# A fused attention and FFN layer: a second ALiBi buffer in place of a third score buffer, and all weight loads on one queue

## What is computed

```python
xn = _layernorm(x)
x = x + attn(xn) + ffn(xn)
# attn, H=16 heads of D=64, T=2048
q, k, v = split(xn @ W_attn + b_attn)
att = (q @ k.T) / sqrt(D) / temperature
att = att + where(causal, slopes[h] * (pos_k - pos_q), -inf)
y = softmax(att) @ v
attn = y @ W_proj + b_proj
# ffn, HIDDEN=3072, int32 weights scaled by 1/127
ffn = (silu(xn @ wg.T) * (xn @ wu.T)) @ wd.T
```

## Time and profile before

| | us |
|---|---|
| time, median of 3 runs | 2096.98 (2095.66 to 2149.68) |
| time of the profiled execution | 2096.67 |
| its span on the slowest core, core 7 | 2095.1 |
| spans of the eight cores | 2070.9 to 2095.1 |
| stage 4 on core 7, from the first score matmul | 1077.9 to 2095.1 |
| TensorE busy on core 7 | 1344.0 |
| VectorE busy | 947.5 |
| ScalarE busy | 923.0 |

### The profile page before, as it was taken

One profiled execution on the slowest core, in us unless ns is written; L12 is line 12 of the kernel. 1 busy time (PEld: TensorE's weight loads), 2 busy tenths in 40 slices (PEclk: granted clock), 3 DMA queues, 4 the chain that ended last, 5 costly groups with the idle time before them and its releaser, 6 DMA issues.

```text
span 2095.1 us, 26200 instructions; the slowest of 8 cores (2070.9 to 2095.1 us)
## 1 busy us (share of the span) xinstructions
PE 1344.0 (64%) x8642; PEld 700.7 (33%) x8642; DVE 947.5 (45%) x1601; ACT 923.0 (44%) x1745; POOL 78.8 (4%) x148
## 2 busy tenths in 40 slices
PE   0000059899898998089976566656656565666666
PEld 0000024344343443034334334334334343432333
DVE  2335321010110110244138686868768686855663
ACT  2335333022031230000248786877777676853442
POOL 0000000000000000023000000000000000000000
PEclk9955579999999999589985555555555555557877
DMA  8878544244243431722210101010100101012212
GB/s 241 269 259 266 169 151 141 81 147 135 77 165 101 133 128 41 257 74 77 85 41 1 61 1 61 1 61 1 51 11 1 61 1 61 1 71 81 81 61 91
DMA packets 46188, 198.87 MB, mean 95 GB/s; under 512 B 6119, under 2 KB 6120, under 8 KB 38378
## 3 DMA queue, kind: packets, MB, share of 16 engines
q1 hardware_dynamic: 31402, 142.67, 21.3%
q0 software_dynamic: 14080, 48.24, 6.3%
q10 hardware_dynamic: 576, 6.29, 0.8%
HBM read 157.34 MB, written 39.85 MB: 94 GB/s over the span
## 4 chain that ended last, share of the span: by engine, by line
PE 50%; DMA 16%; DVE 12%; issue 12%; ACT 9%; DVEq 0%; SPq 0%; ACTq 0%; POOL 0%; POOLq 0%
PE ps_dn L405 8%; PE ps_g L361 8%; PE ps_u L369 8%; PE ps_tr L775 7%; DVE snegp L663 6%; PE ps_qk L492 5%; ACT ptb L739 4%; ACT pbuf L699 4%; PE ps_y L800 4%; PE ps_tr L876 3%; PE ps_v L528 3%; DMA abcp<-alibi_bc 3%; PE ps_s L644 3%; DMA wistage<-wd_r 2%; DVE ncmx L625 2%
## 5 line engine op out<-in xcount | busy, mean ns | idle before, releaser
L663 DVE SCALAR_TENSOR_TENSOR snegp<-ps_s,abcp 128x1024 f32<-128x1024 f32 (+2 forms) x320 | 330.6, 1058 | 246.6 <-PE ps_s L650 246.6
L739 ACT ACTIVATE ptb<-ps_tr 128x512 bf16<-128x512 f32 (+3 forms) x640 | 313.4, 531 | 265.9 <-PE ps_tr L775 261.2
L775 PE MATMUL ps_tr<-ident_s,pbuf 128*128 128x128 bf16 x2176 | 290.1, 296 | 186.8 <-ACT ptb L739 90.1
L625 DVE TENSOR_REDUCE ncmx<-snegp 128x2 f32<-128x1024 f32 (+2 forms) x320 | 328.4, 1052 | 3.5
L699 ACT ACTIVATE pbuf<-snegp,negmax 128x128 bf16<-128x128 f32 (+15 forms) x256 | 305.2, 1195 | 41.1 <-DVE negmax L680 38.9
L775 PEld LDWEIGHTS ps_tr<-ident_s,pbuf 128*128 128x128 bf16 x2176 | 191.4, 128 | 303.3 <-issue 292.3
L644 PE MATMUL ps_s<-k_hp,q_hp 64*128 64x512 bf16 (+2 forms) x320 | 142.8, 506 | 162.1 <-DVE snegp L663 94.4
L405 PE MATMUL ps_dn<-wdres,hbuf 128*128 128x512 bf16 x768 | 177.0, 391 | 38.4 <-DVE xfout L426 32.9
L361 PE MATMUL ps_g<-xnT,wgbuf 128*128 128x512 bf16 x768 | 182.8, 381 | 8.7 <-DMA wubuf<-wu_sc 7.8
L295 PE MATMUL ps<-ident_s,xn_st 128*128 128x128 bf16 x128 | 16.2, 305 | 263.7 <-DVE xn_st L278 263.7
L369 PE MATMUL ps_u<-xnT,wubuf 128*128 128x512 bf16 x768 | 181.4, 379 | 0.0
(11 more groups left out here) (65 smaller groups left out, 1030.0 us busy)
## 6 DMA issues: line engine op xcount, KB each, us to landing
wgbuf<-wg_sc SPq DMA_DIRECT2D x48, 512.0 KB
wubuf<-wu_sc SPq DMA_DIRECT2D x48, 512.0 KB
abcp<-alibi_bc SPq DMA_DIRECT2D x16, 1024.0 KB
wistage<-wg_r SPq DMA_DIRECT2D x12, 1024.0 KB
wistage<-wu_r SPq DMA_DIRECT2D x12, 1024.0 KB
wistage<-wd_r SPq DMA_DIRECT2D x12, 1024.0 KB
xstage<-xin SPq DMA_DIRECT2D x16, 512.0 KB
x2st<-xin POOLq DMA_DIRECT2D x16, 512.0 KB, 5.4
```

The source lines that it names most:

```text
L625: cd = S.op("vector", lambda e, par=par, c0=c0, w=w, ci=ci: e.tensor_reduce(ncmx[:, par * 8:par * 8 + 8].rearrange("p (j c) -> p j c", j=2 ...
L663: stt = S.op("vector", lambda e, par=par, hb=hp % 2, aoff=aoff, c0=c0, w=w, rA=rA: e.scalar_tensor_tensor(snegp[par].rearrange("p (j t) -> ...
L739: return e.activation(dst, src, AF.Copy)
L775: lasttr = S.op("tensor", lambda e, par=par, j=j, kc=kc, slot=slot, idx=idx, n=len(kcs): e.matmul(ps_tr[:, slot * 512 + (kc % 4) * 128: sl ...
```

## The change

Four edits.

- All eight wattn loads are issued on SP; the ScalarE queue and its two semaphores go.
- `snegp` has two buffers instead of three, by s % 2. The addition of step s waits for the exp of s-2 instead of s-3. The small tiles (ncmx, negmax, sumr, rsum) stay with three.
- `abcp` has two buffers, by hp % 2. The load of pair hp waits for the last addition recorded for the buffer's former pair, hp-2.
- The early load of q and k of the first pair waits for all stores of q and k and for `p3_pe`, the last V matmul. The tensors have moved by 16 KB in SBUF.

```diff
-                    ld = S.dma("sync" if wb == 0 else "scalar",
-                        lambda e, dc=dc, wb=wb: e.dma_start(
+                    ld = S.dma("sync", lambda e, dc=dc, wb=wb: e.dma_start(
                         out=wst3[wb][:, :], in_=wattn[dc * 128:(dc + 1) * 128, :]),
...
-            snegp = [E4b(nc.sbuf_tensor(f"snegp{p}", [128, 2 * T], F32, side="right")) for p in range(3)]
+            snegp = [E4b(nc.sbuf_tensor(f"snegp{p}", [128, 2 * T], F32, side="right")) for p in range(2)]
...
-            sneg_rel = [0, 0, 0]
+            sneg_rel = [0, 0]
...
                 if early:
                     wts = [wat_fin, qk_st_war[2], qk_st_war[3]]
-                    wq = [wat_fin] + store_of_fc[0] + store_of_fc[8]
+                    wq = qk_st_fin + [("pe", p3_pe)]
                 else:
-                    wts = [("v", abc_war[0])]
+                    wts = [("v", abc_war[hb])]
...
-                l1 = S.dma("sync", lambda e, hp=hp: e.dma_start(
-                    out=abcp0[:, 0:T], in_=alibi_bc[2 * hp, :, :]), waits=wts)
+                l1 = S.dma("sync", lambda e, hp=hp, hb=hb: e.dma_start(
+                    out=abcp[hb][:, 0:T], in_=alibi_bc[2 * hp, :, :]), waits=wts)
...
-                    if sneg_rel[par]:
-                        wts2.append(("a", sneg_rel[par]))
+                    if sneg_rel[sp]:
+                        wts2.append(("a", sneg_rel[sp]))
...
-                    abc_war[0] = S.c("v")
+                    abc_war[hp % 2] = S.c("v")
...
-                sneg_rel[par] = ed
+                sneg_rel[pb] = ed
...
-            abcp0 = E4b(nc.sbuf_tensor("abcp0", [128, 2 * T], F32, side="right"))
-            abcp = [abcp0, abcp0]
+            abcp = [E4b(nc.sbuf_tensor(f"abcp{i}", [128, 2 * T], F32, side="right")) for i in range(2)]
```

More of the change, by code:

```diff
@@ L29 @@
 class KB:
-    QSEMS = {"sync": ("dl0", "dl1"), "gpsimd": ("dg0", "dg1"),
-             "scalar": ("ds0", "ds1")}
+    QSEMS = {"sync": ("dl0", "dl1"), "gpsimd": ("dg0", "dg1")}
     def __init__(self, nc, block, sem):
@@ L40, in __init__ @@
         self.waited = {e: {} for e in ENGS}
-        self.qidx = {"sync": 0, "gpsimd": 0, "scalar": 0}
+        self.qidx = {"sync": 0, "gpsimd": 0}
     def dma(self, queue, fn, waits=()):
@@ L120, in build_program @@
         sem = {s: E(nc.semaphore("sem_" + s)) for s in
-               ("dl0", "dl1", "dg0", "dg1", "ds0", "ds1", "pe", "v", "a")}
+               ("dl0", "dl1", "dg0", "dg1", "pe", "v", "a")}
         block = E(nc.Block())
@@ L551, in build_program @@
             E4b = s4b.enter_context
-            snegp = [E4b(nc.sbuf_tensor(f"snegp{p}", [128, 2 * T], F32, side="right")) for p in range(3)]
-            sneg = [[snegp[p][:, j * T:(j + 1) * T] for j in range(2)] for p in range(3)]
+            snegp = [E4b(nc.sbuf_tensor(f"snegp{p}", [128, 2 * T], F32, side="right")) for p in range(2)]
+            sneg = [[snegp[p][:, j * T:(j + 1) * T] for j in range(2)] for p in range(2)]
             pbuf = [[E4b(nc.sbuf_tensor(f"pbuf{p}_{j}", [128, T], BF16, side="right")) for j in range(2)] for p in range(2)]
@@ L600, in emit_group_load @@
                     wq = [("pe", qk_war[hb])] if qk_war[hb] else []
-                l1 = S.dma("sync", lambda e, hp=hp: e.dma_start(
-                    out=abcp0[:, 0:T], in_=alibi_bc[2 * hp, :, :]), waits=wts)
-                l2 = S.dma("sync", lambda e, hp=hp: e.dma_start(
-                    out=abcp0[:, T:2 * T], in_=alibi_bc[2 * hp + 1, :, :]))
+                l1 = S.dma("sync", lambda e, hp=hp, hb=hb: e.dma_start(
+                    out=abcp[hb][:, 0:T], in_=alibi_bc[2 * hp, :, :]), waits=wts)
+                l2 = S.dma("sync", lambda e, hp=hp, hb=hb: e.dma_start(
+                    out=abcp[hb][:, T:2 * T], in_=alibi_bc[2 * hp + 1, :, :]))
                 l3 = S.dma("sync", lambda e, hp=hp, hb=hb: e.dma_start(
@@ L614, in emit_scores_softmax @@
                 par = it % 3
+                sp = it % 2
                 ch = chunks_of(L)
@@ L624, in emit_red @@
                     ci, c0, w, dep = pend_red.pop(0)
-                    cd = S.op("vector", lambda e, par=par, c0=c0, w=w, ci=ci: e.tensor_reduce(
+                    cd = S.op("vector", lambda e, par=par, sp=sp, c0=c0, w=w, ci=ci: e.tensor_reduce(
                         ncmx[:, par * 8:par * 8 + 8].rearrange("p (j c) -> p j c", j=2)[:, :, ci:ci + 1],
-                        snegp[par].rearrange("p (j t) -> p j t", j=2)[:, :, c0:c0 + w],
+                        snegp[sp].rearrange("p (j t) -> p j t", j=2)[:, :, c0:c0 + w],
                         AX.X, AluOpType.max),
@@ L659, in emit_scores_softmax @@
                         wts2 += group_ld[hp % 2][0:2]
-                    if sneg_rel[par]:
-                        wts2.append(("a", sneg_rel[par]))
+                    if sneg_rel[sp]:
+                        wts2.append(("a", sneg_rel[sp]))
                     aoff = T - 128 + c0 - qt * 128
-                    stt = S.op("vector", lambda e, par=par, hb=hp % 2, aoff=aoff, c0=c0, w=w, rA=rA: e.scalar_tensor_tensor(
-                        snegp[par].rearrange("p (j t) -> p j t", j=2)[:, :, c0:c0 + w],
+                    stt = S.op("vector", lambda e, sp=sp, hb=hp % 2, aoff=aoff, c0=c0, w=w, rA=rA: e.scalar_tensor_tensor(
+                        snegp[sp].rearrange("p (j t) -> p j t", j=2)[:, :, c0:c0 + w],
                         ps_s[:, rA:rA + 1024].rearrange("p (j t) -> p j t", j=2)[:, :, 0:w],
@@ L699, in emit_exp @@
                     ed = S.op("scalar", lambda e, par=par, pb=pb, j=j, L=L: e.activation(
-                        pbuf[pb][j][:, 0:L], sneg[par][j][:, 0:L], AF.Exp,
+                        pbuf[pb][j][:, 0:L], sneg[pb][j][:, 0:L], AF.Exp,
                         bias=negmax[:, par * 2 + j: par * 2 + j + 1],
```

## The result

The changed kernel takes 2056.31 us as the median of ten executions, the kernel before 2097.69 (ten, taken beside them). The ratio is 0.9795, 95% interval 0.9781 to 0.9809: 2.05% faster. The forecast was 2059 us. On either side some executions are several per cent longer whatever the kernel does; all ratios leave these out, a median over all executions does not. The two medians alone stand at 0.9803, so which side of 2% the gain falls on is not settled.

A forecast was written before the change was run, and what follows sets the result against it. The prediction took ScalarE's idle at seven pair changes, with scores waiting for k, as the loss to remove: 2096.67 - 40.9 + 5.0 - 2.0 = 2058.8, so 2059 us, range about 2050 to 2070.

The forecast's parts named there:

- The stall at the change of pair: Seven pair changes in attention: second abcp buffer removes the k_hp waits and most of ScalarE's idle, gaining 40.9 us.
- snegp: Bias additions in attention: with two buffers the wait for exp(s-2) is already covered by VectorE's earlier reciprocals, cost 0.
- The price without cover: Rival in attention: additions wait for the previous step's exp, exposing up to 305.2 us, up to 2364 us; chance 3%.
- The start: Start of attention: q and k of pair 0 wait for the last V matmul, delaying the first score, cost 5.0 us.
- wattn: W_attn loads all on SP: second load follows sooner (-1.4 us), loads then 4.9 us apart; -2 us in all.
- The 2% mark: Whole run: faster by over 2% begins below 2055 us, given 27%; within 2% given 70%.
- The differences between cores gone: Sign expected in the profile: first to last score about 925 to 928 us on every core, without differences between cores.
- The clock rival: TensorE in attention: without the 9.3 us holes its clock rises to 2.4 GHz, at most 115 us, 1944 us; chance 3%.

The follow-up runs named there:

- e3: The changed kernel with a single abcp buffer again, addresses kept by an unused tile: 2097.75 us, ratio 1.0004 to the kernel before.
- e4: The kernel before, with q and k issued on SP ahead of the two ALiBi loads in each pair's load: 2055.95 us, ratio 0.9804.
- e9: e4, with q and k of the next pair also waiting for the last addition: ratio 0.986 to the kernel before (0.982 to 0.990).
- e10: The changed kernel run once more, unaltered, beside e11 and e12: ratio 0.9831 to the kernel before.
- e5: The changed kernel with tiles reordered so q and k of pair 0 load during V: 2054.87 us, ratio 0.981 to the kernel before.
- e11: e5 run again, unaltered, beside e10: ratio 0.9842 to the kernel before.
- e12: e4 with all wattn loads on SP: ratio 0.9812 to the kernel before.
- e1: The kernel before with two snegp buffers instead of three, addresses kept by an unused tile: ratio 1.0005 to the kernel before.
- e6: The changed kernel with a single snegp buffer: 2240.13 us in a single execution.

## Why the prediction was right, by its steps

- *The stall at the change of pair.* Its mechanism held at each point: seven waits for k gone, ScalarE idle 0.53 us instead of 6.1 to 7.2, TensorE still idle before the transposes (3.29 us). e3 brings the stall back, e4 and e9 show that the path ran through exp, transposes and copies and that TensorE's idle as such was free. The size was 40.9 forecast from core 7. ScalarE's idle at the seven changes fell by 40.9 as a mean over cores, and the attention stretch by 42.6. The six kernels with the short attention and an unchanged body (changed, e10, e4, e5, e11, e12) lie at 927.8 to 930.7, so the 1.7 us are within what the column scatters, and whether anything stands behind them is open. That the stall is paid in full was argued from two cores, whose times less their waits for k both come to 902 us. Over all eight cores that difference runs from 899.6 to 904.3, and the time rises by some 0.65 us for each us of wait, so the agreement of those two was in part luck. What carries the point is that the time came back when the idle went.
- *snegp*: cost 0, as e1 shows. The price without cover was bounded at 305 us; e6 gives 184 to 189.
- *The start*: 5.0 forecast, 4.4 measured. The first score comes 5.4 to 6.3 us after the last V matmul; on core 6 that is 5.9 us after q was issued (1077.43), between the 4.8 and 6.5 of the rows used as bounds.
- *wattn*: -2 forecast, -2.0 measured, with the wrong division. The second load gives -2.6 and not -1.4, since it follows the first not in 5 us but in 4.3, and the 6.4 of core 7 was 6.8 as a mean. The loads after it were to gain 0.1 us each from a two-buffer cycle of 4.9, and they lose 0.1. The term came out right by luck, as two errors cancelled. The Trainium skill ("DMA: Bandwidth & Descriptors", section "Issuing engines are not separate DMA queues") says that DMAs of several engines interleave and that spreading them saves only issue time. The first part doesn't show here for the first two loads: ScalarE's did not share with SP's but stood until it was through.
- *The 2% mark.* The forecast gave 27% to more than 2%. The measured 2.05% has the mark inside its interval (1.91 to 2.19%).
- *"The differences between cores gone"* was too much. First to last score was 965 to 972 us and is 922.7 to 927.8 (925 to 928 was forecast). The order of cores by stall is gone, a spread of 5 us remains.
- *The clock rival.* From the start of attention to 1820 us, core 6 has a granted clock of 0.54, where the kernel before had 0.53 on the same core, and 0.52 to 0.56 on the eight. TensorE remains at 1.2 GHz almost throughout. Closing the holes of 9.3 us did not change that; TensorE still has idle stretches of up to 3.7 us there.

## What to carry to other kernels

A stall at a buffer change is worth what the engine at the end of the chain loses, not what the waiting engine shows: 9.5 us of idle TensorE at each change were worth about 6 (42.6 / 7), and in e9 2.5 us of it were worth next to nothing. Before a buffer is doubled, look at the order on the DMA queue: what the next stage needs first (k) stood behind what it needs last (the ALiBi rows), and swapping the two gave the same 2% without 16 KB per partition. A rotation of buffers is as deep as it must be when an instruction already ahead in the same engine's program waits for the same event.

## What was not expected of the hardware

With a 1.5 MB load of SP's queue under way, a load issued from ScalarE 1.2 us later stood in its queue for 5.2 to 6.0 us, on all eight cores, while a second load on SP itself was issued in 0.33 to 0.38 us and landed 2.6 us earlier relative to the first. The later ScalarE loads, issued when SP's was partly through, took 0.33 us. Why the first one stood is open.
